# Seam between two stages: inputs of the dispatch loaded into buffers that stage one no longer needs, first logits computed during the last batch

## The chip, the core and the metric

The kernel runs on one core of a Trainium2 chip. A core has TensorE (matrix products and transposes, reading SBUF and writing PSUM), VectorE, ScalarE and GpSimd for elementwise work, and SyncE (SP), which here issues every DMA. In the profile they are PE (with PEld for its weight loads), DVE, ACT, POOL and SP. The engines run their own instruction lists and meet through semaphores. The metric is the device time of one execution in microseconds, median of three runs.

## The reference, cut to what matters

Input is a tensor of 16 batches, 256 tokens each, 128 features. Four layers follow, each with a residual and a layer norm: a Mamba block, an attention with chosen experts, a linear attention, and a soft mixture of experts. The first three work batch by batch. The fourth mixes over all batches:

```python
x = _layernorm(x + _L0_attn_ref(x, ...))
x = _layernorm(x + _L0_ffn_ref(x, ...))
x = _layernorm(x + _L1_attn_ref(x, ...))
x = _layernorm(x + _L1_ffn_ref(x, phi, W, b))
# _L1_ffn_ref; x is (16, 256, 128), phi (128, 64, 32): 64 experts with 32 slots each
logits = jnp.einsum('bmd,dnp->bmnp', x, phi)
dispatch = jax.nn.softmax(logits, axis=0)          # over the 16 batches
combine = jax.nn.softmax(logits.reshape(bsz, m, n * p), axis=-1)
slots = jnp.einsum('bmd,bmnp->bnpd', x, dispatch)
y = jnp.einsum('bnpd,nde->bnpe', slots, W) + b[None, :, None, :]
out = jnp.einsum('bnpd,bmnp->bmd', y, combine)
```

The softmax of the dispatch runs over the batches, so its first maximum needs the logits of all 16 batches.

## The kernel before, in words

The program has two parts with a barrier of all engines between them, since each is a block of its own (`token_blocks`, `soft_experts`).

**Stage one** (`token_blocks`) takes the batches through the first three layers in software-pipelined slots, written out by hand for each engine: slot t does the Mamba part (a_) of batch t, the first half of the experts' layer (b_) of batch t-1, its outputs (b_out) of batch t-2 and the linear attention (c_) of batch t-3. Y and Z are the last two batches, 14 and 15, whose ends are written out separately after the last slot. The result of a batch, x3, is written by VectorE (`c_x3`, L1429 to L1435), transposed by TensorE (`c_x3t`, L704), copied by ScalarE into x3T (L1071 to L1074), and SP stores both to DRAM (`store`, L368 to L378). Both buffers hold one batch, so each is written again only when the stores before are in. At its end SP waits for all stores (L395).

**Stage two** (`soft_experts`) has a dispatch and a combine. The dispatch goes through 16 blocks s of 128 slots, each in two halves c of 128 tokens per batch; g = 2s + c numbers the half blocks. For each half block

- `logits(s, c)` on TensorE (L1959 to L1973): 16 products of 128x128 f32, one for each batch, into the four PSUM banks of `lg`; in the profile each such product is two records, so x32;
- `copies` on ScalarE (L2073 to L2082): four copies of these banks into `raw`, which SP stores (`store_raw`, L1851) for the combine;
- `shifted` on VectorE (L2178 to L2193): the maximum over the batches, then two subtractions into `ex`;
- `exps` on ScalarE (L2084), in two halves; `summed` on GpSimd (L2278), four additions over the batches; `scaled` on VectorE (L2195), a reciprocal and a product;
- `slots(s, u, c, k)` on TensorE (L1975), 16 products into the four banks of `sl`, added up over both halves; then `experts` (L1985), 16 products with W for the block.

`block_of` on each engine sets the order. TensorE's is logits(s, 0), experts of s-2, slots(s-1, 0), logits(s, 1), slots(s-1, 1), experts of s-1. A new logits group may start only when the copies and subtractions of the one before have read the same banks.

At the start of stage two SP issues, in this order: the first 128 columns of phi, the identity, the first halves of x3T in four loads, its second halves, the rest of phi, two loads of W, and x3 (L1896 to L1907). TensorE waits for each part of x3T with a semaphore of its own (`x_in`), and for the rest with `late`.

## Time and profile before

| | |
|---|---|
| median of three runs | 1579.81 us (1579.48 to 1579.84) |
| the profiled execution's own time | 1580.04 us |
| its span, first to last instruction | 1578.1 us |
| TensorE busy | 1438.5 us, 91% of the span |
| VectorE, ScalarE, GpSimd busy | 1214.6, 820.8, 790.4 us |
| TensorE's mean granted clock | 0.974 of full speed |
| last store of stage one issued | at 1066.57 us |
| first logits of stage two | at 1072.87 us |

Times in rows are microseconds from the start of the span. Busy time means that an engine worked on an instruction, waits not counted. TensorE's clock is given as a share of 2.4 GHz: 1.00 is 2.4 GHz, 0.50 is 1.2 GHz. In brackets at the end of a row of a timeline stands the idle time of the engine just before the row and what ended it.

### The profile page before, as it was taken

The numbers are of one execution on the slowest core, as the hardware profiler recorded it, in microseconds if no ns is written. First come the engines' busy times: TensorE is split into PE (matmuls) and PEld (weight loads), VectorE is DVE, ScalarE is ACT, GpSimd is POOL, SyncE is SP. The second block draws the span as 40 slices with busy tenths as digits, with TensorE's granted clock in tenths as the row PEclk, the third lists the DMA queues.
The fourth block names the chain that finished last, engine by engine and source line by source line (L and its number), as shares of the span: only waits on it lengthen the run. The fifth ranks groups of instructions, "written<-read, shape, count | busy, mean of one in ns | idle before, by whom it ended". The sixth has DMA issues, their size and how long they took to land. (4 is left out here: it accounts for less than half of the span.)

```text
span 1578.1 us, 32322 instructions
## 1 busy us (share of the span) xinstructions
PE 1438.5 (91%) x10752; PEld 1261.2 (80%) x10752; DVE 1214.6 (77%) x2335; ACT 820.8 (52%) x1846; POOL 790.4 (50%) x1959
## 2 busy tenths in 40 slices
PE   5588999999999999999999999946999999869997
PEld 4366788788788788788788787836999999869997
DVE  4466798898898898898898887764888888736664
ACT  2234544544544544544544544303777776557774
POOL 0332253553553553553553552222777777557763
PEclk9998999999999999999999999966999999989999
DMA  6000000000000000000000000008676667877782
GB/s 236 7 7 1 8 1 14 15 1 14 15 1 15 15 1 14 15 1 15 15 1 15 8 1 8 8 7 252 171 197 188 185 186 199 254 266 301 300 316 71
DMA packets 140752, 132.10 MB, mean 84 GB/s; under 512 B 7376, under 2 KB 130512, under 8 KB 134096
## 3 DMA queue, kind: packets, MB, share of 16 engines
q1 hardware_dynamic: 140624, 130.50, 26.1%
q8 instruction: 68, 1.11, 0.3%
q14 instruction: 60, 0.49, 0.1%
HBM read 73.85 MB, written 56.62 MB: 83 GB/s over the span
## 5 line engine op out<-in xcount | busy, mean ns | idle before, releaser
L636 PE MATMUL bk<-ve_f,oe 128*128 128x128 f32 x2048 | 275.8, 279 | 0.8 <-DVE ve_f L1360 0.8
L636 PEld LDWEIGHTS bk<-ve_f,oe 128*128 128x128 f32 x2048 | 248.9, 192 | 23.4 <-issue 20.1
L2287 POOL TENSOR_TENSOR d_s<-d_ex 128x1024 f32<-128x1024 f32 x32 | 131.8, 4120 | 100.8 <-ACT d_ex L2087 100.8
L1360 DVE SCALAR_TENSOR_TENSOR ve_f<-ps_m,oT 128x512 f32<-128x512 f32 x248 | 166.3, 678 | 3.7 <-PE bk L636 2.3
L1321 DVE COPY_PREDICATED vals<-oh,bk 128x1024 f32<-128x1024 int32 x112 | 146.6, 1309 | 10.3 <-PE bk L404 8.5
L2037 PE MATMUL d_sl<-d_ex,e_prT 128*128 128x128 f32 x1024 | 136.0, 277 | 8.8 <-POOL d_ex L2304 8.8
L1971 PE MATMUL d_lg<-d_phf,d_xtf 128*128 (+1 forms) x1024 | 128.1, 287 | 14.4 <-DVE d_ex L2191 7.6
L1971 PEld LDWEIGHTS d_lg<-d_phf,d_xtf 128*128 128x128 f32 x1024 | 125.1, 203 | 15.2 <-issue 11.1
L2037 PEld LDWEIGHTS d_sl<-d_ex,e_prT 128*128 128x128 f32 x1024 | 125.4, 193 | 9.0 <-POOL d_ex L2304 9.0
L1981 PE MATMUL d_sl<-d_ex,d_xs 128*128 128x128 f32 x1024 | 121.3, 277 | 5.8 <-DVE d_ex L2202 5.8
L1981 PEld LDWEIGHTS d_sl<-d_ex,d_xs 128*128 128x128 f32 x1024 | 118.4, 194 | 6.2 <-DVE d_ex L2202 6.2
L1024 ACT ACTIVATE ve_f<-bk,r 128x128 f32<-128x128 f32 x128 | 47.3, 370 | 136.8 <-DVE r L1333 136.7
L402 PE MATMUL bk<-veH,x1H 128*128 128x512 f32 x256 | 115.3, 451 | 0.9 <-DVE vals L1321 0.8
L2184 DVE TENSOR_REDUCE d_nm<-d_lg 128x128 f32<-128x2048 f32 x32 | 73.3, 2292 | 50.7 <-PE d_lg L1971 48.6
L63 POOL TENSOR_SCALAR lnB_v<-lnB_mv 128x2 f32<-128x2 f32 x15 | 2.9, 193 | 210.2 <-DVE lnB_mv L328 210.2
L926 ACT ACTIVATE pt<-bk 128x384 f32<-128x384 f32 x128 | 62.6, 495 | 74.2 <-PE bk L574 73.0
L404 PE MATMUL bk<-veH,x1L 128*128 128x512 f32 x256 | 100.7, 393 | 0.0
L403 PE MATMUL bk<-veL,x1H 128*128 128x512 f32 x256 | 100.5, 393 | 0.0
L2139 ACT ACTIVATE e_prT<-d_lg 128x512 f32<-128x512 f32 x128 | 72.4, 595 | 47.4 <-PE d_lg L2024 47.4
L2304 POOL TENSOR_TENSOR d_ex<-d_ex,e_bias 128x1024 f32<-128x1024 f32 x32 | 74.9, 2370 | 38.6 <-DMA d_ex<-y_slots 38.6
L2082 ACT ACTIVATE d_raw<-d_lg 128x512 f32<-128x512 f32 x128 | 71.6, 602 | 34.9 <-PE d_lg L1971 17.8
L1200 DVE SCALAR_TENSOR_TENSOR cacc<-cin,cw,cacc 128x256 f32<-128x256 f32 x192 | 86.2, 493 | 3.1 <-ACT cin L926 3.0
(340 smaller groups left out, 3730.5 us busy)
## 6 DMA issues: line engine op xcount, KB each, us to landing
logits<-d_raw SPq DMA_DIRECT2D x128, 256.0 KB, 3.3
e_lt<-logits SPq DMA_DIRECT2D x32, 1024.0 KB, 5.1
y_slots<-d_ys SPq DMA_DIRECT2D x64, 256.0 KB, 4.3
d_ex<-y_slots SPq DMA_DIRECT2D x16, 1024.0 KB, 6.8
d_w<-W SPq DMA_DIRECT2D x16, 256.0 KB, 3.4
oe<-xT SPq DMA_DIRECT2D x1, 2048.0 KB, 7.9
xt_in<-xT SPq DMA_DIRECT2D x16, 128.0 KB, 2.3
x_in<-x SPq DMA_DIRECT2D x16, 128.0 KB, 2.4
```

Source lines behind the costliest of these rows:

```text
L402: pe.matmul(ps, lh, rh, start=first, stop=False, skip_group_check=True)
L403: pe.matmul(ps, lh, rl, start=False, stop=False, skip_group_check=True)
L404: return pe.matmul(ps, ll, rh, start=False, stop=last, skip_group_check=True)
L636: last = pe.matmul(ps_u[:, cols], oe[:, hp, e, :], mo[:, n % MO, hp, :], start=False, stop=(e == NE - 1 and hp == HP - 1), skip_group_chec ...
L1200: V.scalar_tensor_tensor(cacc[:, ch, :], cin[:, ch, tap:tap + L], cw[:, ch, tap:tap + 1], cacc[:, ch, :], ALU.mult, ALU.add).then_inc(q["a ...
L1321: V.copy_predicated(vals[:], oh[:, :, :, e:e + 1].bitcast(I32).to_broadcast([P, C, HB, DH]), ps_v[e % 2][:].rearrange("p c (h k) -> p c h ...
L1360: V.scalar_tensor_tensor(mo[:, n % MO, :, :].rearrange("p a n -> p (a n)"), chosen_of(b, c), float(NE - e), oT[:, u, c, :, :].rearrange("p ...
L1971: last = pe.matmul(lg[:, k, i, :], xtf[:, b, c, :], phf[:, cols], start=(i == 0), stop=(i == BB - 1), skip_group_check=True)
L1981: last = pe.matmul(sl[:, k, i, :], xs[:, (BK * i + k) * C + c, :], ex[:, u, c, k, i, :], start=(c == 0 and i == 0), stop=(c == C - 1), ski ...
L2037: last = pe.matmul(po[:, c, :], prT[:, c, s, :], yb[:, v, s, :], start=(s == 0), stop=(s == SB - 1), skip_group_check=True)
L2287: G.tensor_tensor(s8[:], part[:, 0:8, :], part[:, 8:16, :], ALU.add).then_inc(n, 1)
L2304: G.tensor_tensor(yb[:, v, rows, :], yb[:, v, rows, :], bias[:, rows, :], ALU.add).then_inc(e["y"], 1)
```

## The change

- Fifteen buffers of stage one that its last part (from batch 15's x1 on) does not use become parts of one tensor, `arena`. Its first 10,240 elements per partition are at the same time x3T of all batches (`xtf`), x3 of all batches (`xs`) and phi (`phf`), which were tensors of stage two.
- When batch 15's x1 has been read, SP loads phi there, and after the store of batch 12 also x3T and x3 of batches 0 to 12. The stores of batches 13 to 15 are gone: VectorE and ScalarE write their x3 and x3T into `xs` and `xtf` themselves.
- The eight PSUM banks are two tensors of four banks in both stages, so that `lg` is there during stage one. The linear attention of batch Z works in ps_m instead of a bank of `lg`.
- `logits_ahead` computes the logits of half block 0 during batch Z: twelve products before Z's transposes, three after Y's x3T, the last after Z's.
- In stage two, half block 1 goes to the banks of `sl` (`home_of`). The first blocks are written out: ScalarE does the two last copies of half block 0 behind its exponentials, and VectorE no longer waits for copies before the first two maxima. SP stores `raw` of block 0 when all four copies of a half block are there.

```diff
+    HELD = NB - 3
+    AREAS = dict(cin=(NCH, L + TAPS - 1), cacc=(NCH, L), xbc=(NCH, L), am=(C, NH, P), lx=(C, NH, P), mx=(C, NH, P),
+                 xd=(C, NH, HD), xD=(C, NH, HD), tz=(C, DI), sz=(C, DI), ya=(C, DI), yg=(C, DI), yT=(2, L),
+                 xt_in=(2, L), x_in=(2, C, D))
+    arena = kept.enter_context(nc.sbuf_tensor("arena", [P, sum(math.prod(shape) for shape in AREAS.values())], F32))
...
+    two = [kept.enter_context(nc.psum_tensor(f"ps_{n}", [P, 4, 512], F32)) for n in "ls"]
...
+        def x3_of(b, c):
+            return xs[:, C * b + c, :] if b >= HELD else x3[:, c, :]
...
-            for b in range(NB - 5, NB):
+            for b in range(NB - 5, HELD):
                 store(b)
-            sp.wait_ge(x3_stored, 32 * NB)
+            sp.wait_ge(q["a_x1h"], NB)
+            sp.wait_ge(q["a_x1l"], NB)
+            sp.dma_start(phf[:, 0:S], phi).then_inc(held_in[0], 16)
+            sp.wait_ge(x3_stored, 32 * HELD)
+            sp.dma_start(xtf[:, 0:HELD, :, :], x3T_dram.rearrange("p (b c t) -> p b c t", c=C, t=P)[:, 0:HELD, :, :]
+                         ).then_inc(held_in[1], 16)
+            sp.dma_start(xs[:, 0:C * HELD, :], x3_dram.rearrange("(n p) d -> p n d", p=P)[:, 0:C * HELD, :]
+                         ).then_inc(held_in[2], 16)
+            for n in range(3):
+                sp.wait_ge(held_in[n], 16)
...
+            def logits_ahead(k, i):
+                if (k, i) == (0, 0):
+                    pe.wait_ge(held_in[0], 16)
+                    pe.wait_ge(held_in[1], 16)
...
+                b = BK * i + k
+                if b >= HELD:
+                    pe.wait_ge(q["c_x3t"], b + 1)
+                last = pe.matmul(lg[:, k, i, :], xtf[:, b, 0, :], phf[:, 0:P], start=(i == 0), stop=(i == BB - 1),
+                                 skip_group_check=True)
+                if i == BB - 1:
+                    last.then_inc(lg_ps, 1)
...
             c_out(Y)
+            for k in range(BK):
+                for i in range(BB - 1):
+                    logits_ahead(k, i)
             b_x2t(Z, 1)
...
             c_x3t(Y)
+            for k in range(BK - 1):
+                logits_ahead(k, BB - 1)
             c_x3t(Z)
+            logits_ahead(BK - 1, BB - 1)
...
+        def home_of(g):
+            return sl if isinstance(g, int) and g == 1 else lg
...
+            logits(0, 1)
+            logits(1, 0)
+            for k in range(BK):
+                slots(0, 0, 0, k)
+            logits(1, 1)
+            for k in range(BK):
+                slots(0, 0, 1, k)
+            for k in (0, 1):
+                experts(0, 0, 0, k)
             pe.wait_ge(ready, READY)
-            block_of(0, 0, one=False, two=False)
-            pe.wait_ge(late, 32)
-            block_of(0, 1, two=False)
...
+            act.wait_ge(q["max"], 1)
+            first_copies(0, (2, 3))
+            exps(0, 0, 0, 0)
+            exps(0, 0, 0, 1)
+            first_copies(0, (0, 1))
+            act.wait_ge(q["max"], 2)
+            first_copies(1, (2, 3))
+            act.wait_ge(q["sub"], 3)
+            first_copies(1, (0, 1))
+            exps(0, 0, 1, 0)
+            exps(0, 0, 1, 1)
+            copies(1, 0, (0, 1))
+            copies(1, 0, (2, 3))
+            exps(1, 1, 0, 0)
+            exps(1, 1, 0, 1)
+            copies(1, 1, (0, 1))
+            copies(1, 1, (2, 3))
+            slots(0, 0)
+            slots(0, 1)
...
```

**TensorE at the transposes of batch Z's x2** (L652 before, L682 now; the rows ahead of them are batch Y's last products). Before:

```order
L698 MATMUL ps_c<-kv,qr 128x128
L700 MATMUL ps_c<-kmh,ql 128x16
L652 MATMUL ps_o<-id_f,x 128x128 [waits lnB_rows]
L652 MATMUL ps_o<-id_f,x 128x128
L663 MATMUL bk<-x2T,wl 128x256 [waits b_pt,b_x2t]
```

Now (ps_l is the tensor behind `lg`, ps_s the one behind `sl` and the small banks; L750 is `logits_ahead`):

```order
L728 MATMUL ps_s<-kv,qr 128x128
L730 MATMUL ps_s<-kmh,ql 128x16
L750 MATMUL ps_l<-arena 128x128 [waits b_mo,b_pt,b_oa,held_turned,held_phi]
L750 MATMUL ps_l<-arena 128x128 x11
L682 MATMUL ps_s<-id_f,x 128x128 [waits lnB_rows]
L682 MATMUL ps_s<-id_f,x 128x128
L693 MATMUL ps_s<-x2T,wl 128x256 [waits b_mo,b_x2t]
```

Twelve products of the logits stand between Y's last products and Z's transposes, with the waits for the loaded inputs on the first.

**TensorE across the barrier.** L707 and L737 are the transposes of x3, L1971 and L2022 the logits of stage two. Before:

```order
L707 MATMUL ps_c<-id_f,x 128x128 [waits c_x3]
L707 MATMUL ps_c<-id_f,x 128x128
L707 MATMUL bk<-id_f,x 128x128 [waits c_x3]
L707 MATMUL bk<-id_f,x 128x128
L106 UNCONDITIONAL_BRANCH
L1957 UNCONDITIONAL_BRANCH [waits barrier_Pool_Activation_PE_DVE_SP_release]
L1971 MATMUL d_lg<-d_phf,d_xtf 128x128 [waits d_x_in0,d_ready]
L1971 MATMUL d_lg<-d_phf,d_xtf 128x128 x3
L1971 MATMUL d_lg<-d_phf,d_xtf 128x128 [waits d_x_in1]
L1971 MATMUL d_lg<-d_phf,d_xtf 128x128 x3
```

Now:

```order
L750 MATMUL ps_l<-arena 128x128
L750 MATMUL ps_l<-arena 128x128 [waits c_x3t] x2
L737 MATMUL ps_s<-id_f,arena 128x128 [waits c_x3]
L737 MATMUL ps_s<-id_f,arena 128x128
L750 MATMUL ps_l<-arena 128x128 [waits c_x3t]
L127 UNCONDITIONAL_BRANCH
L2007 UNCONDITIONAL_BRANCH [waits barrier_Pool_Activation_PE_DVE_SP_release]
L2022 MATMUL ps_s<-arena 128x128 x16
L2022 MATMUL ps_l<-arena 128x128 [waits d_sub,d_raw]
L2022 MATMUL ps_l<-arena 128x128 x3
```

The logits of half block 0 have left stage two; behind the barrier TensorE starts with the 16 products of half block 1, which wait for nothing, and then waits for half block 0's copies and subtractions.

**SP across the barrier.** The x_tok and x_T rows are the stores of x3 and x3T. Before, after batch Z:

```order
L374 DMA x_tok<-x 128x2x128 [waits c_x3,x_all_in]
L378 DMA x_T<-x3T 128x256 [waits c_x3t,x_all_in]
L106 UNCONDITIONAL_BRANCH [waits x3_stored]
L1841 UNCONDITIONAL_BRANCH [waits barrier_Pool_Activation_PE_DVE_SP_release]
L1896 DMA d_phf<-phi 128x128
L1897 DMA d_id<-ident 128x128
L1901 DMA d_xtf<-x_T 128x4x128 x4
L1902 DMA d_xtf<-x_T 128x16x128
L1904 DMA d_phf<-phi 128x1920
L1849 DMA d_w<-W 128x512 [waits d_ready] x2
L1907 DMA d_xs<-x_tok 128x32x128
```

Now, after batch 12:

```order
L395 DMA x_tok<-x 128x2x128 [waits c_x3,x_all_in]
L399 DMA x_T<-x3T 128x256 [waits c_x3t,x_all_in]
L418 DMA arena<-phi 128x2048 [waits a_x1l,a_x1h]
L420 DMA arena<-x_T 128x3328 [waits x3_stored]
L422 DMA arena<-x_tok 128x26x128
L127 UNCONDITIONAL_BRANCH [waits held_rows,held_turned,held_phi]
L1900 UNCONDITIONAL_BRANCH [waits barrier_Pool_Activation_PE_DVE_SP_release]
L1955 DMA d_id<-ident 128x128
L1908 DMA d_w<-W 128x512 [waits d_ready] x2
L1917 DMA logits<-d_raw 128x4x128 [waits d_raw,d_ready]
```

Three loads have moved ahead of the barrier and eight have left stage two's start; the stores of logits follow directly on the loads of W.

## Rows read from the trace of the kernel before

**Rows 1.** Busy time by stretch: stretch, its us, each engine's busy us, TensorE clock.
```profile
160.00:1010.00 850.00, 823.93 (x5937) 683.99 (x5936) 727.92 (x1677) 421.59 (x1192) 405.62 (x1394) 1.00 0.03 9
1036.00:1038.00 2.00, 0.00 (x0) 0.00 (x0) 1.83 (x8) 0.00 (x0) 0.00 (x0) 0.93 0.00 0
1039.00:1054.00 15.00, 9.82 (x26) 5.88 (x26) 5.24 (x15) 1.70 (x5) 8.14 (x32) 0.50 0.00 1
1108.00:1200.00 92.00, 92.00 (x824) 92.00 (x825) 80.28 (x51) 65.45 (x102) 69.42 (x42) 1.00 0.68 184
```

**Rows 2.** The chain of waits across the seam: start us, us, what.
```profile
1069.58 3.15 DMA d_xtf<-x_T
...
1072.87 6.59 PE d_lg L1971 x32
...
1079.48 2.30 DVE d_nm L2184
...
1081.81 1.24 DVE d_ex L2191
...
1104.65 0.95 DVE d_sr L2199
...
1107.97 3.84 PE d_sl L1981 x32
```

**Rows 3.** SP's timeline, end of stage one: start us, us, what.
```profile
960.08 0.33 SPq L378 DMA_DIRECT2D x_T<-x3T  x1
...
1066.57 0.33 SPq L378 DMA_DIRECT2D x_T<-x3T  x1
...
1068.71 0.34 SPq L1896 DMA_DIRECT2D d_phf<-phi  x1
```

**Rows 4.** TensorE's timeline, last batches: start us, us, line, operation, idle before.
```profile
1023.74 0.38 PE L652 MATMUL ps_a<-id_f,x 128*128 128x128 f32 x2
...
1024.85 1.03 PE L663 MATMUL ps_c<-x2T,wl 128*128 128x256 f32 x4
...
1034.33 0.29 PE L700 MATMUL ps_c<-kmh,ql 128*128 128x16 f32 x2
...
1039.36 0.69 PE L652 MATMUL ps_o<-id_f,x 128*128 128x128 f32 x2 [4.74 <-DVE x L339]
...
1040.53 2.07 PE L663 MATMUL bk<-x2T,wl 128*128 128x256 f32 x4 [0.47 <-ACT x2T L926]
```

**Rows 5.** ScalarE's timeline: Z's x3T copy, first half block of stage two.
```profile
1066.11 0.38 ACT L926 ACTIVATE x3T<-bk 128x256 f32<-128x256 f32 x1 [8.10 <-PE bk L707]
...
1081.87 1.08 ACT L2082 ACTIVATE d_raw<-d_lg 128x512 f32<-128x512 f32 x2 [4.61 <-DVE d_nm L2184]
...
1082.97 1.28 ACT L2087 ACT_TABLE_LOAD   x1
...
1084.27 2.00 ACT L2087 ACTIVATE d_ex<-d_ex 128x1024 f32<-128x1024 f32 x2
```

**Rows 6.** DMA issues over the whole run: count, KB each, median us to landing.
```profile
logits<-d_raw SPq DMA_DIRECT2D x128, 256.0 KB, 3.3
...
x_T<-x3T SPq DMA_DIRECT2D x16, 128.0 KB, 1.7
...
d_id<-ident SPq DMA_DIRECT2D x1, 64.0 KB, 1.9
...
d_xs<-x_tok SPq DMA_DIRECT2D x1, 0.5 KB, 13.3
```

**Rows 7.** GpSimd's timeline: the sum of half block 0, start of the next.
```profile
1086.44 2.35 POOL L2287 TENSOR_TENSOR d_s<-d_ex 128x1024 f32<-128x1024 f32 x1 [33.95 <-ACT d_ex L2087]
...
1091.01 0.45 POOL L2294 TENSOR_TENSOR d_sm<-d_s 128x128 f32<-128x128 f32 x1
...
1095.69 4.17 POOL L2287 TENSOR_TENSOR d_s<-d_ex 128x1024 f32<-128x1024 f32 x1 [4.22 <-ACT d_ex L2087]
```

**Rows 8.** DMA queues from 1066 to 1076 us: packets, MB, share.
```profile
q1 hardware_dynamic: 3431, 1.76, 59.9%
```

More of the change, by code:

```diff
@@ L102, in token_blocks @@
                  ident, causal, neg_blocks, strict_low, upper, head_of, rot, cosT, sinT, w8,
-                 x3_dram, x3T_dram, x3_stored):
+                 x3_dram, x3T_dram, x3_stored, phi):
+    HELD = NB - 3
[3 more added lines that the diff above has]
+    arena = kept.enter_context(nc.sbuf_tensor("arena", [P, sum(math.prod(shape) for shape in AREAS.values())], F32))
+    area, at = {}, 0
+    for name, shape in AREAS.items():
+        part = arena[:, at:at + math.prod(shape)]
+        at += math.prod(shape)
+        area[name] = (part.rearrange("p (a b) -> p a b", a=shape[0]) if len(shape) == 2 else
+                      part.rearrange("p (a b c) -> p a b c", a=shape[0], b=shape[1]))
+    xtf = arena[:, 0:NB * L].rearrange("p (b c t) -> p b c t", b=NB, c=C)
+    xs = arena[:, NB * L:2 * NB * L].rearrange("p (n d) -> p n d", n=TT)
+    phf = arena[:, 2 * NB * L:2 * NB * L + S]
+    two = [kept.enter_context(nc.psum_tensor(f"ps_{n}", [P, 4, 512], F32)) for n in "ls"]
+    lg, sl = (ps[:, :, :].rearrange("p k (b s) -> p k b s", b=BB) for ps in two)
+    lg_ps = kept.enter_context(nc.semaphore("d_lg_ps"))
+    held_in = [kept.enter_context(nc.semaphore(f"held_{n}")) for n in ("phi", "turned", "rows")]
     with ExitStack() as ctx:
@@ L1072, in c_x3t @@
                 act.wait_ge(q["c_x3t_ps"], b + 1)
-                wait(act, x3_stored, 32 * b)
-                copy(x3T[:], linear_of(b)[:, 0:L]).then_inc(q["c_x3t"], 1)
+                if b >= HELD:
+                    act.wait_ge(q["a_x1l"], NB)
+                else:
+                    wait(act, x3_stored, 32 * b)
+                copy(xtf[:, b, :, :].rearrange("p c t -> p (c t)") if b >= HELD else x3T[:], linear_of(b)[:, 0:L]).then_inc(q["c_x3t"], 1)
             act.wait_ge(ready, READY)
@@ L1817, in soft_experts @@
         ready = sem("d_ready")
-        late = sem("d_late")
-        x_in = [sem(f"d_x_in{k}") for k in range(BK + 1)]
         loads = [sem(f"d_loads{v}") for v in range(YB)]
@@ L1977, in slots @@
                 pe.wait_ge(q["mult"], 2 * (C * s + c + 1))
-                if c == 0:
-                    wait(pe, q["ys"], BK * (s - 1) + k + 1 if not isinstance(s, int) or s else 0)
+                if c == 0 and isinstance(s, int) and s == 0:
+                    pe.wait_ge(q["raw"], BK * C)
+                elif c == 0:
+                    pe.wait_ge(q["ys"], BK * (s - 1) + k + 1)
                 for i in range(BB):
@@ L2151, in batch @@
                     turned(b + 1, 0, (2, 3))
-            block_of(0, 0, one=False, two=False)
-            block_of(0, 1, two=False)
+            act.wait_ge(q["max"], 1)
[17 more added lines that the diff above has]
+            slots(0, 1)
+            exps(1, 1, 1, 0)
+            exps(1, 1, 1, 1)
+            slots(0, 2)
+            slots(0, 3)
+            outputs(0, 0, 0, 0)
+            outputs(0, 0, 0, 1)
             for u in range(2):
@@ L2178, in shifted @@
             def shifted(g, s, u, c):
[L2180 removed]
+                whole = home_of(g)[:, :, :, :].rearrange("p k b s -> p (k b) s")
                 dve.wait_ge(q["lg_ps"], BK * (g + 1))
[L2182 removed]
+                if not (isinstance(g, int) and g < C):
+                    dve.wait_ge(q["raw"], BK * g + 2)
                 wait(dve, q["sub"], 2 * g)
```

120 lines of the change are left out of this document (60 added, 60 removed).

## The prediction

> **What bounds the kernel now.** I read four views in this order. The table of busy time by stretch comes first: from 1108 to 1200 us TensorE is busy for 92.00 of 92 us at full clock [rows 1], so once the dispatch runs, every microsecond in the program is TensorE's, and whatever brings the start of that stretch forward brings the end forward. The chain of waits comes second, to find where that stretch starts: at 1107.97, with the second half of the slots of block 0 (the 32 records of the slots' line) [rows 2]. Before it the chain alternates: a load of x3T (3.15 us), logits of one half block (6.59 us), a maximum (2.30), a subtraction (1.24), logits again, three such rounds, and at the end reciprocal and scaling, 1104.65 to 1107.97, which is 3.3 us [rows 2]. TensorE waits here because all logits share one set of four PSUM banks. Third is SP's timeline: the last store of stage one is issued at 1066.57, the first load of stage two at 1068.71 [rows 3], and the logits begin only at 1072.87. Fourth, TensorE's own timeline of the last batch: it stands idle for 4.74 us from 1034.6 to 1039.36 [rows 4]. So from the end of ScalarE's last x3T copy (1066.11 + 0.38 = 1066.5, [rows 5]) to the continuous stretch at 1107.97 there are 41.5 us, in which TensorE does four groups of half-block work and mostly waits. That is the stretch which the change rewrites.
>
> **The change part by part.**
>
> *Loads moved ahead.* phi, x3T and x3 of 13 batches are issued by SP after the store of batch 12. The x3T store of that batch was issued at 960.08 [rows 3]. The worst landing of such loads was 13.3 us, for x3 [rows 6]; three of them one after the other are 40 us, so they are in by about 1000, and the first reader is TensorE at 1034.6. Cost nothing; the cover is some 34 us. Nothing else of SP's queue is behind them, since the stores of the last three batches are gone. If the cover were gone, TensorE's queue would stop before the last batch's transposes, microsecond for microsecond.
>
> *The last three batches written in place.* Same instructions, another destination: nothing on VectorE and ScalarE. Their waits for earlier stores released nothing late before (both last VectorE rows ran without a wait).
>
> *Twelve logits during the last batch.* Sixteen cold logits take 6.59 us, 0.41 each; at full clock 3.84 (the slots' row, same shape), 0.24 each [rows 2]. Twelve are 2.9 us warm, 4.9 cold. They start at 1034.6, when the clock is still full: the granted clock fell only inside 1036 to 1038 (mean 0.93) [rows 1]. So they end at 1037.5, before the transposes at 1039.36: hidden. If cold, they would delay these by 0.2 us. They also shorten the idle stretch ahead of the transposes from 4.74 to 1.9 us. Before, everything from 1039 to 1054 ran at 0.50, 9.82 us of TensorE work [rows 1], all of it on the last batch's chain. The same transposes take 0.38 us warm and 0.69 cold, the q and k products 1.03 and 2.07 [rows 4]. Bounds: a loss of 0.2 us to a gain of 4.9 (all of the 9.82 halved). I take 1.0: after the last matmul of before (1034.6) the clock was still full at 1036 and most of the way to 1038; the same again after 1037.5 covers the transposes (0.31 saved) and most of the q and k products (1.04), and after that TensorE is busy for under half of the time.
>
> The Trainium skill (TensorE: Matmul & The Clock Gate, HAM oscillation) says that a long idle gap between bursts brings the slow clock back. This case's trace agrees for 4.74 us of idle. By that rule alone, no gap after 1037.5 being as long, the whole chain could stay warm; that is a rival below.
>
> *The seam.* Before: x3T store issued 1066.57, landing 1.7 us later [rows 6] at 1068.3, first instruction behind the barrier 1068.71: the barrier costs 0.4. Now nothing is stored or loaded there. The last work is one logits matmul on the copied x3T: 1066.5 + 0.5 = 1067.0. With the barrier, all engines start at T = 1067.4; with the clock gain, 1066.4.
>
> *From T to the continuous stretch.* The logits of half block 0 are ready at T.
> - VectorE's maximum starts at T. Before, from the start of the same maximum (1079.48) to the end of GpSimd's sum (1091.01 + 0.45) were 12.0 us [rows 2, 7], with two copies (1.08), the table load (1.28) and the exponentials (2.00) between them [rows 5]. The same steps in the same order: sum 0 at T+12.0.
> - TensorE meanwhile computes half block 1 into the other four banks, cold, T to T+6.6. VectorE follows: maximum to 8.9, two subtractions to 11.4 (2.30 + 2 × 1.2). It is free when sum 0 arrives; scaling 0 runs 12.0 to 15.3.
> - Half block 2 needs the banks of half block 0: the last two copies, moved behind the exponentials, end at 6.8 + 1.1 = 7.9. Logits 2 run 7.9 to 14.5 even cold. Not on the path.
> - Slots of the first half: from 15.3, 3.8 us warm or 6.6 cold. Then logits 3, 3.6 to 3.8 warm, whose banks are free at about 20 (maximum and subtractions of half block 2 from 15.3).
> - Sum 1: ScalarE's exponentials of half block 1 end at 11.4 + 2.1 = 13.5; the sum takes 4.17 + 2.67 = 6.8 (its first addition is the slower 4.17, as VectorE scales beside it) [rows 7]: 20.4. Scaling 1: to 23.7. Slots of the second half can start then, or when logits 3 are out: 19.1 + 3.8 = 22.9 with both warm, 21.9 + 3.6 = 25.5 with the slots cold. So T+23.7 to T+25.5; I take 24.3.
> - The four copies of logits to SBUF for half block 2 wait for SP's stores of half block 0: issued from T+8 at intervals of half a microsecond, landing 3.3 us after issue [rows 6], the last at T+13.3; wanted at 13.5.
> - Behind the slots, ScalarE's two slot copies now stand after two logits copies that wait for maximum 3 (23.7 + 2.3). They end at 28.4 instead of the 27.4 at which TensorE's experts would start: 0.5 us more. Everything later is in the old order.
>
> Sum: 1066.4 + 24.3 + 0.5 = 1091.2 takes the place of 1107.97. Gain 16.8 us. The profiled execution took 1580.04 us (span 1578.1 and 1.9 around it), so 1563.2; it stood 0.2 above the median of the runs, hence **1563.0**. Its own range is 1560.5 to 1565.5: 0 to 2.5 for the clock in the last batch and -0.6 to +1.7 for the start of the slots.
>
> **The rivals.**
> 1. *The clock stays full through the last batch's chain.* For: the idle gap that let it fall is filled. Against: at 1.2 GHz TensorE was busy 9.82 of 15 us there, at 2.4 it would be a third. Gain 3.9 us beyond the 1.0 taken: 1559.1.
> 2. *The restart is not free.* Before, every engine's first work behind the barrier was hidden by 4 us and more of loads. Now three engines need their first instructions of the new stage at once. Against: between 1066 and 1076 only the data queue moved packets, no instruction queue [rows 8]. A fetch that had to be waited for would cost at least the shortest load, 1.9 us [rows 6], and on VectorE and ScalarE in sequence twice that: 1565 to 1567. The Trainium skill (Runtime: NRT & Kernel Launch, Instruction fetch mechanics) says that a taken branch may need its target fetched before the engine goes on. By that rule the seam would show such a gap; no row of before can show one, since the loads hide it.
> 3. *The new order gives part back.* If the slots and logits 3 both run cold (28.4 instead of 24.3), or SP's stores of half block 0 land late, TensorE's stretch starts 2 to 4 us later: 1565 to 1567.
> 4. *Slower than before.* Fifteen buffers of stage one now lie in one arena, at other addresses and in another neighbourhood. TensorE is busy for 823.93 of 850 us there and VectorE for 727.92 [rows 1]. If these places make the operations of stage one slower, each of 16 batches pays. From 1.05 us per batch (16.8 / 16, about 2% of a batch) the change loses; at 2 us per batch it ends at 1595. For: nothing in the trace; the same kinds of operand, in the same memory.
> 5. *It does not do what it says:* the ahead logits are pushed behind the chain by a late load. The loads would have to take 70 us instead of 13.3.
>
> **How the numbers follow.** Forecast 0.62; rival 1 0.12; rival 2 0.12; rival 3 0.09; rival 4 0.04; rival 5 0.01. About 0.2% (3.2 us) is what can be told from no change here. All but rivals 4 and 5 are faster by far more: faster 0.95, same 0.01, slower 0.04. The range leaves out rival 4 and 5 and the far tail of rivals 1 to 3: 1558.8 to 1567.3.
>
> **What would show it.** Twelve logits between 1034.6 and 1037.5 with the transposes not later than 1039.4; the first maximum of stage two within 0.6 us of the last logits matmul; scaling 0 ending 15.3 us after that maximum's start; second-half slots 23.7 to 25.5 after it, and from there no idle TensorE until the drain. Wrong if a gap of 2 us and more opens behind the barrier, if stage one's batches before 1030 have moved, or if TensorE idles after the second-half slots.

## The result, and the profile after

The changed kernel took 1568.45 us (median of 4 runs, 1564.97 to 1569.71) against 1579.78 us (median of 4); the ratio on record is 0.9923, 95% interval 0.9908 to 0.9937. It is faster, by 11.3 us instead of 16.8, and lies 1.1 us above the range. The profiled execution took 1569.71 us, the longest of the four, span 1568.0.

Busy time by stretch (engines in the order PE, PEld, DVE, ACT, POOL, then TensorE's clock, the DMA share, GB/s) answers to [rows 1]:

```profile
160.00:1010.00 850.00, 823.78 (x5922) 682.85 (x5921) 729.97 (x1675) 420.98 (x1192) 403.15 (x1395) 1.00 0.05 14
1036.00:1038.00 2.00, 1.64 (x14) 1.64 (x15) 1.72 (x12) 0.00 (x0) 0.00 (x0) 1.00 0.00 0
1039.00:1054.00 15.00, 8.20 (x30) 4.78 (x30) 7.99 (x25) 1.69 (x5) 8.26 (x32) 0.71 0.01 2
1098.00:1200.00 102.00, 101.43 (x909) 101.27 (x908) 88.57 (x58) 75.07 (x118) 73.23 (x46) 1.00 0.70 182
```

Stage one is what it was. The second-half slots, with which the dense stretch began before, start at 1095.05 instead of 1107.97, 12.9 us earlier; one wait of 0.57 us follows them (below). SP's timeline shows the three loads right behind the last x3T store, at 963 to 965, and no load of them at the seam [rows 3]:

```profile
962.90 0.33 SPq L399 DMA_DIRECT2D x_T<-x3T  x1
963.33 0.39 SPq L418 DMA_DIRECT2D arena<-phi  x1
964.75 0.32 SPq L420 DMA_DIRECT2D arena<-x_T  x1
965.27 0.80 SPq L422 DMA_DIRECT2D arena<-x_tok  x1
1069.52 0.35 SPq L1955 DMA_DIRECT2D d_id<-ident  x1
```

TensorE's timeline across the seam, with the idle time before a group in brackets, answers to [rows 2, 4]:

```profile
1037.27 2.92 PE L750 MATMUL ps_l<-arena 128*128 128x128 f32 x24
1042.17 0.44 PE L682 MATMUL ps_s<-id_f,x 128*128 128x128 f32 x2 [1.97 <-DVE x L360]
1043.08 1.13 PE L693 MATMUL ps_s<-x2T,wl 128*128 128x256 f32 x4 [0.47 <-ACT x2T L977]
1045.23 1.22 PE L700 MATMUL ps_s<-wl,x2T 128*128 128x128 f32 x4 [1.02 <-ACT wk_f L1115]
...
1068.44 0.79 PE L750 MATMUL ps_l<-arena 128*128 128x128 f32 x2 [0.47 <-ACT arena L977]
1069.56 5.21 PE L2022 MATMUL ps_s<-arena 128*128 128x128 f32 x32 [0.32 <-PEq L127]
1077.30 3.84 PE L2022 MATMUL ps_l<-arena 128*128 128x128 f32 x32 [2.53 <-ACT d_raw L2145]
1086.23 5.41 PE L2034 MATMUL ps_s<-d_ex,arena 128*128 128x128 f32 x32 [5.09 <-DVE d_ex L2289]
1091.48 3.74 PE L2022 MATMUL ps_l<-arena 128*128 128x128 f32 x32
1095.05 3.74 PE L2034 MATMUL ps_s<-d_ex,arena 128*128 128x128 f32 x32
1099.36 2.02 PE L2043 MATMUL ps_s<-d_w,d_slot 128*128 128x128 f32 x16 [0.57 <-ACT d_slot L2155]
```

The twelve logits (24 records, 2.92 us) fill what was a hole of 4.74 us; the transposes and the q and k products behind them run at full speed (0.44 and 1.13 us, before 0.69 and 2.07), the v products at half speed again (1.22), though TensorE was never idle for more than 1.97 us between the logits and them. The barrier shows 0.32 us of idle, and between 1066 and 1076 us no instruction queue moved a packet. But the first slots take 5.41 us where 3.84 is full speed. VectorE and GpSimd, ahead of those slots, answer to [rows 2, 5, 7]:

```profile
1069.55 2.29 DVE L2271 TENSOR_REDUCE d_nm<-ps_l 128x128 f32<-128x2048 f32 x1 [2.33 <-PEq L127]
...
1081.55 0.95 DVE L2286 RECIPROCAL d_sr<-d_sm 128x128 f32<-128x128 f32 x1 [2.06 <-POOL d_sm L2386]
1082.53 3.64 DVE L2289 TENSOR_TENSOR d_ex<-d_ex,d_sr 128x2048 f32<-128x2048 f32 x1
```

```profile
1081.06 0.45 POOL L2386 TENSOR_TENSOR d_sm<-d_s 128x128 f32<-128x128 f32 x1
1081.69 2.34 POOL L2379 TENSOR_TENSOR d_s<-d_ex 128x1024 f32<-128x1024 f32 x1 [0.17 <-POOL d_sm L2386]
1084.10 3.19 POOL L2381 TENSOR_TENSOR d_s<-d_s 128x512 f32<-128x512 f32 x1
```

Sum 0 ends at T+12.0 (T, the first maximum, is 1069.55), as worked out. The scaling then takes 3.64 us instead of 2.29: GpSimd's first addition of sum 1 began 0.8 us before it and ended at 1084.03, and the product ends 2.14 us after that. GpSimd's next addition, behind the product, takes 3.19 us instead of 1.26.

**Where the time went, leg by leg.** The same five instructions were read in each profile: the first store of x3 (SP), the last batch's transposes (TensorE, idle 1.97 us before it above), the second-half slots, the dispatch's last slots, and the combine's first products with the expert outputs. The columns give each leg's change in us, of after against the first profile of before; of the other pairs below likewise.

| Pair | to first x3 store | to last batch's transposes | to second-half slots | to last slots | to combine's products | to the end | span |
|---|---|---|---|---|---|---|---|
| forecast | 0 | 0 | -17.3 | +0.5 | 0 | 0 | -16.8 |
| after, before | +2.2 | +0.6 | -15.7 | +0.9 | +1.5 | +0.5 | -10.1 |
| e1 (after again), before | 0.0 | +0.3 | -14.5 | +0.8 | +1.7 | +0.6 | -11.1 |
| e10, e12 (start-up filled in both) | -0.5 | +0.5 | -14.2 | +1.3 | +1.5 | +0.5 | -10.9 |

The forecast's -17.3 is 1107.97 - 1039.36 = 68.6 becoming 1090.7 - 1039.36 = 51.3; its +0.5 is the experts' wait. So four things are missing: 1.6 to 3.1 us in the seam, 2.4 to 2.8 us behind it where the forecast had nothing more, 0.3 to 0.6 us between the first store and the transposes, and in one profile 2.2 us of start-up. The largest part behind the seam is in the drain, the end of the dispatch. TensorE's timeline there, after and then before:

```profile
1363.85 6.49 PE L2034 MATMUL ps_s<-d_ex,arena 128*128 128x128 f32 x32 [5.49 <-DVE d_ex L2289]
1388.87 2.08 PE L2090 MATMUL ps_s<-d_ex,e_prT 128*128 128x128 f32 x8 [8.38 <-POOL d_ex L2396]
```

```profile
1375.89 5.33 PE L1981 MATMUL d_sl<-d_ex,d_xs 128*128 128x128 f32 x32 [5.31 <-DVE d_ex L2202]
1399.45 2.08 PE L2037 MATMUL d_sl<-d_ex,e_prT 128*128 128x128 f32 x8 [8.80 <-POOL d_ex L2304]
```

From the one row to the other are 25.02 us after and 23.56 before. Not every profile of the new order shows this loss; all of them are compared in the section on the prediction.

### The profile page after: what moved, and what is told of

It is laid out like the page before. It is cut to its first block and busy times, and to the rows that moved or that the text cites. A ratio compares the mean times of both kernels' runs of the same rounds, so it can differ in the third digit from the quotient of the medians.

```text
span 1568.0 us, 32309 instructions
## 1 busy us (share of the span) xinstructions
PE 1438.7 (92%) x10752; PEld 1260.9 (80%) x10752; DVE 1217.9 (78%) x2335; ACT 819.8 (52%) x1846; POOL 786.0 (50%) x1959
## 3 DMA queue, kind: packets, MB, share of 16 engines
q1 hardware_dynamic: 135008, 128.92, 26.5%
## 5 line engine op out<-in xcount | busy, mean ns | idle before, releaser
L666 PE MATMUL ps_l<-ve_f,oe 128*128 128x128 f32 x2048 | 275.9, 279 | 0.8 <-DVE ve_f L1414 0.8
L666 PEld LDWEIGHTS ps_l<-ve_f,oe 128*128 128x128 f32 x2048 | 249.0, 192 | 23.3 <-issue 20.1
L1414 DVE SCALAR_TENSOR_TENSOR ve_f<-ps_s,oT 128x512 f32<-128x512 f32 x248 | 166.4, 679 | 3.7 <-PE ps_l L666 2.3
L1375 DVE COPY_PREDICATED vals<-oh,ps_l 128x1024 f32<-128x1024 int32 x112 | 146.8, 1311 | 10.8 <-PE ps_l L434 8.7
L2090 PE MATMUL ps_s<-d_ex,e_prT 128*128 128x128 f32 x1024 | 136.5, 278 | 8.4 <-POOL d_ex L2396 8.4
L2034 PE MATMUL ps_s<-d_ex,arena 128*128 128x128 f32 x1024 | 124.0, 281 | 10.6 <-DVE d_ex L2289 10.6
L2090 PEld LDWEIGHTS ps_s<-d_ex,e_prT 128*128 128x128 f32 x1024 | 125.8, 194 | 8.6 <-POOL d_ex L2396 8.6
L2034 PEld LDWEIGHTS ps_s<-d_ex,arena 128*128 128x128 f32 x1024 | 121.1, 198 | 11.0 <-DVE d_ex L2289 11.0
L432 PE MATMUL ps_l<-veH,x1H 128*128 128x512 f32 x256 | 115.7, 452 | 0.9 <-DVE vals L1375 0.8
L2022 PE MATMUL ps_l<-arena 128*128 (+1 forms) x960 | 112.2, 275 | 2.5 <-ACT d_raw L2145 2.5
L2022 PEld LDWEIGHTS ps_l<-arena 128*128 128x128 f32 x960 | 109.6, 192 | 2.7 <-ACT d_raw L2145 2.7
```

Of the source, the lines that this page charges most:

```text
L432: pe.matmul(ps, lh, rh, start=first, stop=False, skip_group_check=True)
L666: last = pe.matmul(ps_u[:, cols], oe[:, hp, e, :], mo[:, n % MO, hp, :], start=False, stop=(e == NE - 1 and hp == HP - 1), skip_group_chec ...
L1375: V.copy_predicated(vals[:], oh[:, :, :, e:e + 1].bitcast(I32).to_broadcast([P, C, HB, DH]), ps_v[e % 2][:].rearrange("p c (h k) -> p c h ...
L1414: V.scalar_tensor_tensor(mo[:, n % MO, :, :].rearrange("p a n -> p (a n)"), chosen_of(b, c), float(NE - e), oT[:, u, c, :, :].rearrange("p ...
L2022: last = pe.matmul(home_of(g)[:, k, i, :], xtf[:, b, c, :], phf[:, cols], start=(i == 0), stop=(i == BB - 1), skip_group_check=True)
L2034: last = pe.matmul(sl[:, k, i, :], xs[:, (BK * i + k) * C + c, :], ex[:, u, c, k, i, :], start=(c == 0 and i == 0), stop=(c == C - 1), ski ...
```

## The experiments

**The same kernel again** (e1_same), no edit.

> The changed kernel itself, again, to see how far its own times spread and what differs between two profiles of it. Its profiled execution shows a shift of 2.2 us against the kernel before in the stretch from 116 to 249 us, where both have the same instructions: TensorE's granted clock was 0.50 from 125 to 130 us there and 0.84 before. Theory clock: the granted clock falls at other moments in each execution, so the times of this kernel spread over 3 to 5 us again, and a second profile shows the first x3 store (249.18 us) earlier or later by 1 us or more, with the difference in rows of 120 to 145 us. Rival arena: the new places of the buffers cost it, then the shift of 2.2 us stands in every profile of this kernel, within 0.3 us, and the times lie at 1568 to 1570.

Measured: 1567.24 us (1566.01 to 1570.06, 5 runs), ratio 0.9921 [0.9907, 0.9934]. Its profile had the start-up of before (first store at 246.98, before 247.01, after 249.18) and is the second line of the table: the start-up's 2.2 us are not part of the change, the rival (the arena's places cost them) is out, and without them the seam and the drain are still short. The runs behind this and the later experiments were taken on three chips, on which the kernel before had medians of 1580.39 (e1 to e4), 1578.79 (e5 to e8) and 1581.04 us (e9 to e12). So medians of different groups are compared with some 2 us of doubt, and the readings below rest on the profiles.

**Without the logits ahead** (e2_no_ahead): loads ahead, writing in place, the second set of banks and the order of stage two stay.

```
-            for k in range(BK):
-                for i in range(BB - 1):
-                    logits_ahead(k, i)
...
+            logits(0, 0)
             logits(0, 1)
```

> One part undone: no logits of half block 0 during batch Z; TensorE computes them at the start of stage two, ahead of half block 1. The loads of 13 batches, the last three written in place, the two sets of banks and the order of stage two stay. Theory: the first maximum then starts 5.2 to 6.6 us behind the barrier instead of at once, the last batch's chain loses the 1.2 us that a full clock gave its first two items, and one product less stands before the barrier (0.8 us): 5.5 to 7.5 us more than the changed kernel, some 1574 to 1576. Rival: the seam's gain is all in the loads and TensorE's logits would be hidden behind other work anyway: 0 to 2 us more, 1568 to 1570.

Measured: 1573.02 us (1571.46 to 1579.22, 4 runs), ratio 0.9952 [0.9937, 0.9968]. So 5.8 of the 13.2 us that e1 gained on this chip are the logits computed ahead, within the 5.5 to 7.5 expected. The rest comes with what stays: the loads and stores that left the seam, the second set of banks and the new order of stage two; no run parts these. In its profile the last batch's chain is back at half speed (0.69 and 2.07 us), and the seam leg is -8.3 us: 6.5 from the transposes to the first maximum (33.6 us instead of 40.1) and 1.8 behind it.

**GpSimd's second sum waits for the first scaling** (e3_sum_waits).

```
                 pool.wait_ge(q["ex"], 2 * (g + 1))
+                if isinstance(g, int) and g == 1:
+                    pool.wait_ge(q["mult"], 2)
```

> GpSimd's first addition of half block 1 waits until VectorE has scaled half block 0; nothing else differs from the changed kernel. In the changed kernel's profile VectorE's first scaling product took 3.64 us instead of 2.29, while GpSimd's addition had started 0.8 us before it, and GpSimd's second addition took 3.19 instead of 1.27. Theory: the two engines take turns on SBUF, and the one that comes second waits; then the product takes 2.29 again, the first slots start 16.7 - 1.35 = 15.3 us behind the first maximum, and 1.3 us are gained, if the clock is the same, with sum 1 still in time (ends before VectorE's second reciprocal starts). Rival: the product is slow for another reason (the store DMAs that run at full rate beside it, 283 GB/s): it stays at 3.6 us and the time gains nothing or loses, since sum 1 comes 3 us later.

Measured: 1565.08 us (1564.89 to 1566.99, 4 runs), ratio 0.9905 [0.9890, 0.9920]. VectorE's timeline:

```profile
1081.18 2.29 DVE L2289 TENSOR_TENSOR d_ex<-d_ex,d_sr 128x2048 f32<-128x2048 f32 x1
...
1089.79 4.05 DVE L2289 TENSOR_TENSOR d_ex<-d_ex,d_sr 128x2048 f32<-128x2048 f32 x1
```

and GpSimd's:

```profile
1083.71 2.35 POOL L2381 TENSOR_TENSOR d_s<-d_ex 128x1024 f32<-128x1024 f32 x1 [3.55 <-DVE d_ex L2289]
...
1089.33 2.35 POOL L2381 TENSOR_TENSOR d_s<-d_ex 128x1024 f32<-128x1024 f32 x1 [0.57 <-ACT d_ex L2150]
1091.77 3.19 POOL L2383 TENSOR_TENSOR d_s<-d_s 128x512 f32<-128x512 f32 x1
```

The scaling is back at 2.29 us, so its length was the meeting with GpSimd and the rival (the stores beside it) is out; the first slots start at T+15.3, the forecast's number. The collision is not gone, it has moved to the second scaling: GpSimd starts at 1089.33 and is done at 1091.68, VectorE's product ends at 1093.84, 2.16 us after that. Second-half slots at T+25.7, against 25.5 and 26.5 in the two profiles without the wait. The expected 1.3 us are not shown: the seam leg is -15.4, between those two, and the interval of the ratio overlaps e1's.

**Products in TensorE's gap ahead of the first slots**, 12 (e4_warm_slots) and 19 (e5_gap_full); nothing reads their results.

```
             logits(1, 0)
+            pe.wait_ge(q["raw"], BK * C)
+            pe.wait_ge(q["sub"], 2 * C)
+            for n in range(19):
+                pe.matmul(sl[:, n % BK, 0, :], xtf[:, n % 12, 0, :], phf[:, 0:P], ...)
```

> Twelve products of no use are added on TensorE into the banks of the second set, in its idle 5 us before the first slots; nothing else differs from the changed kernel. Theory: in the changed kernel the clock fell to 0.50 in that wait (full at 1085, 0.57 at 1086) and the first slots took 5.41 us instead of 3.84; with the wait filled the clock stays full, the slots take 3.8 and the second slots start 1.6 us earlier, unless VectorE's second scaling (ready 24.4 us behind the first maximum) then holds them: gain 1.1 to 1.6 us. Rival: the slots are slow because their weights come from a freshly scaled tile while DMAs run, or the added work itself delays them: 5.4 us as before and no gain.

> Edit: 19 products (4.5 us at full clock, twice what e4 had less a fifth) whose results nothing reads, put between the logits of half block 1 and the first half of the first slots, where TensorE stood idle for 5.6 us. Clock theory (the slots of 5.41, 5.88 and 5.46 us instead of 3.84 are TensorE at the lower granted clock, after its idle stretch): in e4 the products ended 3.0 us before the slots and the clock fell all the same; with under 1.5 us left it stays up, the 32 records of the first slots take 3.8 to 4.2 us, the second half starts at T+24.5 to 25.2 instead of T+26.2 (T is the first maximum), and the median is 1565.5 (1 to 2 below the 1567.24 of the same kernel without them). Rival (the slots are slow because the transfers, at a DMA share of 1.2, and GpSimd take SBUF from their operands): they stay at 5.4 to 5.9 us whatever went before, median 1567 +- 0.7.

Measured: e4 1566.57 us (1565.37 to 1567.97, 4 runs), ratio 0.9918 [0.9903, 0.9933]; e5 1565.99 (1565.45 to 1566.73, 4 runs), 0.9915 [0.9898, 0.9931]. TensorE's timeline of e4, then of e5:

```profile
1077.75 2.84 PE L2110 MATMUL ps_s<-arena 128*128 128x128 f32 x24
1083.61 5.46 PE L2034 MATMUL ps_s<-d_ex,arena 128*128 128x128 f32 x32 [3.01 <-DVE d_ex L2293]
```

```profile
1079.86 4.41 PE L2110 MATMUL ps_s<-arena 128*128 128x128 f32 x38
1085.14 3.84 PE L2034 MATMUL ps_s<-d_ex,arena 128*128 128x128 f32 x32 [0.87 <-DVE d_ex L2293]
1088.81 3.74 PE L2022 MATMUL ps_l<-arena 128*128 128x128 f32 x32
1092.96 3.84 PE L2034 MATMUL ps_s<-d_ex,arena 128*128 128x128 f32 x32 [0.41 <-DVE d_ex L2293]
```

With 3.01 us of idle left the slots were slow as before (5.46), and e4's expectation failed; with 0.87 left they took 3.84. In the 4 us over the slots the granted clock was 0.70 in e4 and 1.00 in e5, beside the same transfers (173 and 165 GB/s). So their length is the clock, and the rival (contention) is out. In e5 the second half starts at T+24.5; the forecast had T+24.3. The median moved as expected in direction, but its interval overlaps e1's.

**Both cures** (e6_wait_and_full): the wait of e3 and the 12 products of e4.

> Edit: both cures of the dispatch's start together: GpSimd's second sum waits for the first scaling (e3), and 12 products fill TensorE's 3.7 us ahead of the first slots. Theory (two separate prices: VectorE's scaling stretched by GpSimd, 4.20 instead of 2.29 us, and the lower clock): first slots at T+15.3 taking 3.8 to 4.2 us. The second half then waits for VectorE, whose second scaling was stretched to 4.05 us in e3, since the sum of half block 2 runs beside it: T+25.6 as in e3, so the median is that of e3, 1565.1 +- 0.7, and filling the gap pays nothing more. Rival (the two prices add in the end time): second half at T+24.3 as forecast, median 1563.3.

Measured: 1569.48 us (1566.45 to 1570.30, 4 runs), ratio 0.9931 [0.9914, 0.9948]. The seam was as the theory had it (first slots at T+15.32 taking 3.84, second half at T+25.67), the median 4 us above it: a miss. TensorE now idled 2.94 us ahead of the second-half slots, and these ran at half speed for the most part (5.30 us): an engine fed too early waits in the next place. That costs 1.5 us. The profile's span is 2.6 us above e3's (1567.8 and 1565.2), and 2.2 of that is its start-up (first store at 250.17, e3 247.97). What else is in the 4 us of the median is not shown.

**Products in the two waits between dispatch and combine** (e7_drain_full), the seam unchanged.

```
+                        for n in range(20):
+                            pe.matmul(lg[:, n % BK, 0, :], ...)
                     for k in range(BK):
                         slots(s - 1, 1 - u, 1, k)
...
                 turn(0, 0, 0, k)
+            pe.wait_ge(q["ys"], BK * SB)
+            for n in range(30):
+                pe.matmul(sl[:, 3, n % BB, :], ...)
```

> Edit: nothing in the seam. 20 products fill TensorE's wait of 5.4 us ahead of the dispatch's last slots, and 30 its wait of 8.2 us ahead of the combine's first products, so that the clock is up at both. Clock theory (the lead of 12 to 13 us shrinks by 1.2 to 1.4 us in the drain, because its last slots took 6.49 and 6.79 us where the kernel before had 5.33): they take 3.8 to 4.3 us, and the first copy of the combine's weights, the load of the expert outputs and its first products come 2.0 to 2.9 us earlier; end time 2.5 us less, median 1564.7. Rival (the combine starts when the stored slots have come back through DRAM, and that time is set by transfers): the slots get faster and the combine starts as late as before, median 1567 +- 0.7.

Measured: 1566.16 us (1564.27 to 1569.06, 4 runs), ratio 0.9911 [0.9894, 0.9927]. TensorE's timeline:

```profile
1365.74 3.84 PE L2034 MATMUL ps_s<-d_ex,arena 128*128 128x128 f32 x32 [1.18 <-DVE d_ex L2298]
1388.73 2.03 PE L2096 MATMUL ps_s<-d_ex,e_prT 128*128 128x128 f32 x8 [2.49 <-POOL d_ex L2405]
```

From the last slots to the combine's products 22.99 us, 2.0 less than after and 0.6 less than before. The slots are 2.65 us shorter than after's and the leg 2.03: most of the clock's cost there is passed on through store, load and GpSimd. Of the 1.5 us that after loses against before, its slower slots (6.49 against 5.33) are 1.2. (Its first store came at 249.61, so the median says less than this leg.)

**Products in every gap of the last batch's chain** (e8_chain_full): rival 1 of the prediction, built.

```
             b_x2t(Z, 1)
+            warm(1)
             c_qk(Z, 1)
+            warm(3)
...
             c_out(Z)
+            warm(12)
...
+            warm(20)
             c_x3t(Z)
```

> Edit: 1 to 20 products in each of TensorE's gaps in the last batch's chain. They keep the clock up, which is rival 1 of the prediction built on purpose. Clock theory: from the first transposes of the last batch to the first maximum 27.6 us become 24.0 (the prediction priced all pieces at full clock at 3.9 less than its own sum), and the median is 1563.7, 3.5 below the 1567.24. Rival (the products stand in front of the chain's own pieces, each of which waits for an engine whose end shifts by some tenths): 26.5 to 28 us, median 1566 to 1568. Another end: because the engine is busy for longer here, the clock falls later, in the first slots, and what is won in the chain is lost there.

Measured: 1565.29 us (1562.30 to 1566.80, 4 runs), ratio 0.9903 [0.9887, 0.9920]. The clock over that chain, in e8, after and before:

```profile
1041.00:1068.00 27.00, 20.62 (x143) 0.95 0.01 2
```

```profile
1042.00:1069.00 27.00, 11.85 (x38) 0.56 0.01 1
```

```profile
1039.00:1066.00 27.00, 11.13 (x30) 0.50 0.03 10
```

From the transposes to T 25.70 us instead of 27.4 to 27.6: the warm chain is worth 1.7 to 1.9 us, half of what rival 1 had been priced at. Part of the gain is lost in waits for other engines: the products behind the v products start 0.5 us sooner than after's, but the next transposes wait for VectorE and start 8.81 us behind the first ones in both profiles.

**The kernel before once more** (e9_before), no edit.

> Edit: none, the kernel before once more, for a second profile of it. Nine profiles of the changed kernel and its variants, the same code up to 1036 us, had the first store of x3 anywhere from 246.0 to 251.1 us (mean 248.7); the one profile of before had 247.0. Theory (the start-up's length is an accident of each execution and of no version): this profile may have it anywhere in 246 to 251 too, the end moves with it by as much, and the nine or so runs of before spread over 3 to 4 us. Rival (before starts up the same way every time, and only the changed kernel's start-up varies, which would be a cost of the change): 247.0 +- 0.3 and runs within 0.5 us.

Measured: 1578.91 us (1577.90 to 1584.04, 10 runs), beside 15 other runs of it with 1581.04 (1578.18 to 1584.32). SP's first store of x3, in this profile, and TensorE's stretch from 120 to 145 us in it:

```profile
251.08 0.38 SPq L374 DMA_DIRECT2D x_tok<-x  x1
```

```profile
120.00:145.00 25.00, 19.70 (x95) 0.64 0.00 1
```

In the first profile of before:

```profile
247.01 0.38 SPq L374 DMA_DIRECT2D x_tok<-x  x1
```

```profile
120.00:145.00 25.00, 19.39 (x109) 0.80 0.00 1
```

The store came 4.07 us later, and the span is 4.0 us longer (1582.1 against 1578.1). ScalarE's same instructions lie 0.35 us apart at 120 us and 3.95 at 148: nearly all of the difference between two executions of one kernel arises where the clock differs. The rival (only the changed kernel varies) is out.

**Products in the start-up's gaps**, in the changed kernel (e10_start_full) and in the kernel before (e12_before_start).

```
+            def heat(t, n):
+                if isinstance(t, int) and t == 1:
+                    for m in range(n):
+                        pe.matmul(ps_c[:, 0:P], id_f[:], id_f[:], ...)
...
                 if a:
+                    heat(t, 6)
                     a_yt(t, more)
```

> Edit: the changed kernel with 29 products that nothing reads in TensorE's gaps in the second slot of stage one (about 110 to 140 us), where the granted clock had fallen to 0.5 to 0.8 in every profile. Clock theory (the first store comes at 246.0 to 251.1 us because the clock falls at another moment each time in that stretch, where it leaves 1.0 in all of them): the clock stays at 1.0 or nearly, the first store comes at 244 to 246 us, the median is 1563.5 (3.5 less), and its runs lie within 2 us instead of the 5 seen. Rival (the spread comes from transfers or from the other engines of the start-up): the store still comes anywhere from 246 to 251 and the median stays at 1567 +- 1.

> Edit: the kernel before with the same 29 products in its start-up. It is the control for e10: with the start-up's accident out of both, the two differ by the change alone. Theory: median 1576 (3 to 4 less than before, 1579.8), and e10 lies 12 to 12.5 below it, the lead that the first pair of profiles had between the first slots and the drain; so the change is worth no 16.8 us even without the start-up's share. Rival (the start-up hid the rest of the forecast gain): e10 lies 15 or more below it.

Measured: e10 1564.92 us (1563.67 to 1566.20, 4 runs), ratio 0.9906 [0.9889, 0.9922]; e12 1575.30 (1574.83 to 1577.37, 6 runs), 0.9971 [0.9959, 0.9984]. The start-up of e10:

```profile
241.64 0.38 SPq L395 DMA_DIRECT2D x_tok<-x  x1
```

```profile
120.00:145.00 25.00, 22.71 (x160) 1.00 0.00 1
```

The clock stays at 1.00 and the first store comes at 241.64 (242.09 in e12), 3.9 to 9.5 us earlier than in the eleven profiles without these products (246.02 to 251.11), earlier than I had expected. (e11, below, has 241.84.) So the spread of the start-up is the clock, and the rival (transfers or other engines) is out. The runs lie within 2.6 us each. The medians fell less: by 2.3 to 3.5 us (from 1567.24 and 1568.45) and by 3.5 to 5.7 (from 1578.79 to 1581.04). The profiled execution was the slowest of its kernel in six of the ten kernels after to e9, so the profiles may show longer start-ups than the median run has; no run shows the others' start-up. e10 is 10.4 us below e12: with the start-up out of both the change is worth 10.4 us, less than the 12 to 12.5 expected, and the rival (15 or more) is out.

**All fillings together** (e11_all_full): e5, e7, e8 and e10 in one kernel.

> Edit: all four fillings together (start-up, the last batch's chain, the gap ahead of the first slots, the two waits of the drain). Theory: their gains add, since each is TensorE at full clock in another place of one chain: 3 us of start-up, 1.9 from the last transposes to the first maximum (27.55 to 25.70 in e8), 2.0 from there to the second half of the first slots (26.5 to 24.5 in e5), and 2.3 from the drain's last slots to the combine (25.25 to 22.99 in e7): median 1558 +- 1.5, better than every kernel so far. Rival (the clock has a budget: what is filled in one place makes it fall soon after in another, as the first slots at 5.97 us in e8 may be read): each gain is given back behind it, median 1563 to 1566.

Measured: 1557.30 us (1554.55 to 1559.78, 4 runs), ratio 0.9860 [0.9838, 0.9882]: better than both kernels, as forecast, and faster than any part alone. Its legs against the first profile of before: -5.2, +0.5, -18.8, +0.7, -0.8, -1.7, in sum the -25.3 of the span (1552.8). TensorE at the dispatch's last slots and at the combine:

```profile
1353.08 3.84 PE L2062 MATMUL ps_s<-d_ex,arena 128*128 128x128 f32 x32 [1.20 <-DVE d_ex L2330]
1375.86 1.16 PE L2124 MATMUL ps_s<-d_ex,e_prT 128*128 128x128 f32 x8 [1.95 <-POOL d_ex L2437]
```

The mean clock is 0.995 (after 0.977). The gains add: 1557.3 against the 1558 expected; the rival of a budget that is spent elsewhere (1563 to 1566) is out. Its four runs are two at 1554.6 to 1554.9 and two near 1559.8; what parts them was not settled.

## Why the prediction was wrong, by its own steps

- **Loads moved ahead, in place, barrier: right.** The loads were issued at 963 to 965 and no reader waited. The barrier cost 0.3 us (0.7 in e2). Rival 2 (a fetch of at least 1.9 us) did not happen. By the rule of the Trainium skill (Runtime: NRT & Kernel Launch, Instruction fetch mechanics) a taken branch may stall on its fetch; no row at this seam shows it. T itself came at 27.4 to 27.6 us behind the transposes, forecast 27.0 (27.9 in e10); 0.3 of that is the last logits product, which took 0.79 us at half speed where the sum had 0.5.
- **Logits ahead: right**, hidden in every profile that has them. **The clock gain: right on the average.** The transposes took 0.44 us each time, but the q and k products 1.13, 1.65 and 1.91 us (after, e1, e10; 2.07 before): a gain of 1.2, 0.7 and 0.4 us, where 1.0 was taken. Rival 1 did not happen by itself, and forced (e8) it pays 1.7 to 1.9 us, not 3.9. Nor was the premise right that no idle stretch after 1037.5 is as long as 4.74 us: TensorE idled for 7.80 us ahead of the last batch's x3 transposes before, and 6.53 after.
- **T to sum 0: right** to the tenth (T+12.0 in every profile of the changed kernel and its variants).
- **Failed: "It is free when sum 0 arrives; scaling 0 runs 12.0 to 15.3."** It ran to 16.6 and 17.2. I had let VectorE start first and GpSimd's addition take the 4.17 us [rows 7]. But the logits of half block 1 ran partly warm (5.21 and 5.94 us, not 6.6), ScalarE's exponentials were done sooner, and GpSimd started at T+12.1 and T+12.7, ahead of VectorE's product at T+13.0, and not at T+13.5: 3.64 to 4.36 us instead of 2.29. The term was 1.3 to 2.0 us short. The Trainium skill (SBUF — State Buffer, SBUF: two separate sides) says that of such a pair whichever starts first holds the shared ports for its whole instruction. The rows agree: each product that GpSimd was ahead of ends 2.1 to 2.2 us after GpSimd's addition does, and in before, where VectorE was ahead, the addition of 4.17 us ends 2.2 us after the product.
- **Failed: slots of the first half at 3.8 us.** They ran after 5.1 to 5.6 us of idle TensorE, at half clock for most of their length: 5.41 and 5.88. The prediction had both ends (23.7 warm, 25.5 cold) and took 24.3, near the warm one, though the nearest rows of before, logits behind idle stretches, were cold:

```profile
1083.13 6.56 PE L1971 MATMUL d_lg<-d_phf,d_xtf 128*128 128x128 f32 x32 [3.69 <-DVE d_ex L2191]
1093.43 6.54 PE L1971 MATMUL d_lg<-d_phf,d_xtf 128*128 128x128 f32 x32 [3.73 <-DVE d_ex L2191]
```

With the idle filled (e5) the second half starts at T+24.5, although the scaling still took 3.66 us. So the late scaling alone leaves the forecast's 24.3 nearly whole, and late and cold slots together make 25.5 and 26.5. That after has just the 25.5 which the prediction gave for cold slots is luck: its slots began 1.4 us later than there and took 1.2 us less.
- **Failed in part: "Everything later is in the old order."** In order, yes. The experts' wait was right (0.57 us for 0.5; the prediction's 28.4 and 27.4 are 1.0 apart, but its 0.5 fits the 24.3 that it took). But the leg to the last slots cost 0.8 to 1.3 us in after, e1 and e10, and 1.5 to 1.7 us were lost from there to the combine. There the drain's slots took 6.49, 6.79 and 6.53 us, against 5.33, 5.47 and 5.37 in before, e9 and e12. e7 shows that it is the clock, and what it costs. It is not a loss of every execution of the new order, though: the six variants with the same drain (e2 to e6, e8) had slots of 5.20 to 5.92 us and 23.8 to 24.6 us from them to the combine, against 23.6 to 23.7 in the three profiles of the old order. Without the slots' own time this leg is 18.5 to 18.6 us in the new order (19.1 in e2) and 18.2 to 18.3 in the old. So 0.3 us stand in every profile, and the rest is how long the clock stays low at the slots in that execution. What sets that, and what makes the 0.3 us, is open.
- **Stage one (rival 4): nearly nothing.** From the first store to the last batch's transposes 792.1 to 792.5 us in three profiles of before and its variant, 792.5 to 793.0 in eleven of the changed kernel and its variants: 0.4 us in 16 batches, not 16.
- **The range.** It has no term for the spread between executions; the old kernel's three runs lay within 0.4 us. Over the ten runs of e9 the same kernel spread over 6 us. A third of the distance to the profiled run (2.2 of 6.5 us) was this. The same changed kernel again (e1) had 1567.24 us, at the range's upper end, so that the median lies above it is in part chance. The missing gain is not: 10.4 to 13.2 us in three comparisons with the old kernel, 16.8 forecast. For the start of the second-half slots the range had +1.7 us where its own cold end gives +1.2; e1 had +2.2.

## What to carry to other kernels

When a wait of several microseconds goes or a new one opens, price the TensorE work behind it at both clock levels and take the level of the nearest row that stands behind an idle stretch of like length; and do so for the later idle stretches, too, whose start moves with the change. Where VectorE and GpSimd work on SBUF at once, as the scaling and the sums do here, ask which starts first, for the instruction that starts second ends almost its own full length behind the first. And before a saving of a few microseconds is believed, read one instruction far ahead of the change in both profiles: if it has moved, the executions differ before the change has acted.

## What the runs showed that I had not expected

- One stretch of 25 us at the start, in which TensorE is busy for 18 to 21 us with gaps of 0.2 to 1.2 us, decides up to 5 us of a 1570 us kernel, differently in each execution: granted clock 0.64 to 0.80, first store 246.0 to 251.1. With 29 products in the gaps the clock is 1.00, the store at 241.6 to 242.1 in both kernels. The mean clock from 120 to 145 us does not order the profiles (e4 has 0.66 and the earliest store); how soon the clock is back does. From 140 to 145 us it was 1.00 in the three with the store at 246.0 to 247.0, 0.90 and 0.69 at 248.0 and 248.4, 0.62 and 0.59 at 249.1 and 249.2, and 0.50 in the four from 249.6 on.
- Idle TensorE time in which the engine only waits for others was not free here: filling it in four places with products that nobody reads (298 more matmul records, +2.8% of them) took the changed kernel from 1567.24 and 1568.45 to 1557.30 us.
